# Feed-forward block and its two norms moved into the stage of the third relational layer; the last norm moved into the graph and attention output stage, both by node tiles

## What is computed

```python
xn = _layernorm(x)
x = x + relational_gnn(xn) + linear_attention_0(xn)     # three relational layers, the last is:
#   h3 = relu(sum_r mean_over_edges_of_r(h2 @ w_rel3[r]) + h2 @ w_root3 + b3), x = x + h3
x = x + ffn(_layernorm(x))       # 768 -> 192 -> 768, new_gelu, weights scaled by mixed coefficients
xn = _layernorm(x)
x = x + graph_conv(xn) + linear_attention_1(xn)         # attention ends in a norm with gamma, beta
x = x + experts(_layernorm(x))   # one shared expert, and two of eight routed ones for each token
```

## Time and profile before

| | us |
|---|---|
| median of three runs | 2197.76 |
| the profiled execution, its own time | 2203.24 |
| its span in the trace | 2201.5 |
| end of `g3` on TensorE to start of `m1` | 943.1 to 1044.2 |
| last graph product of `p1` to start of `rs` | 1382.4 to 1403.5 |

### The profile page before, as it was taken

One profiled execution on the slowest core, in us unless ns is written; L12 is line 12 of the kernel. 1 busy time (PEld: TensorE's weight loads), 2 busy tenths in 40 slices (PEclk: granted clock), 3 DMA queues, 4 the chain that ended last, 5 costly groups with the idle time before them and its releaser, 6 DMA issues. The chain is left out here.

```text
span 2201.5 us, 33777 instructions
## 1 busy us (share of the span) xinstructions
PE 2006.6 (91%) x13496; PEld 1892.4 (86%) x13496; DVE 1327.5 (60%) x1873; ACT 942.4 (43%) x1150; POOL 90.6 (4%) x70
## 2 busy tenths in 40 slices
PE   5899889999999999935999889799979999999996
PEld 4899879999999999935999879699968888888885
DVE  8455566444334343365357646562368888898886
ACT  6345412221222111111366632321157777777775
POOL 0000000000000000000001000000000101001001
PEclk9999899999999999967999979799989999999998
DMA  2310134220211121110310040412279999999997
GB/s 82 102 29 30 58 100 101 67 56 29 84 51 49 51 58 44 44 29 5 105 29 29 1 136 15 165 44 101 72 288 385 383 385 372 369 370 371 372 376 265
DMA packets 186687, 314.00 MB, mean 143 GB/s; under 512 B 13051, under 2 KB 87291, under 8 KB 186160
## 3 DMA queue, kind: packets, MB, share of 16 engines
q1 hardware_dynamic: 181488, 295.70, 38.5%
q0 software_dynamic: 4816, 16.62, 3.3%
q10 hardware_dynamic: 272, 0.07, 0.0%
HBM read 293.87 MB, written 20.40 MB: 143 GB/s over the span
## 5 line engine op out<-in xcount | busy, mean ns | idle before, releaser
L183 PE MATMUL psum<-re_whi,xt_sb 128*128 128x512 f32 (+1 forms) x1680 | 507.8, 377 | 1.5 <-DVE xt_sb L2889 1.5
L183 PE MATMUL psum<-ring_hi,xt_sb 128*128 128x256 f32 (+3 forms) x1920 | 357.5, 285 | 11.9 <-DVE m_v L701 3.9
L183 PEld LDWEIGHTS psum<-re_whi,xt_sb 128*128 128x128 f32 x1680 | 313.1, 189 | 47.1 <-issue 1.9
L2873 DVE TENSOR_TENSOR re_wlo<-moe_raw,re_whi 128x1536 fp32r<-128x1536 f32 x173 | 303.3, 1755 | 34.3 <-ACT re_whi L2827 33.8
L183 PEld LDWEIGHTS psum<-ring_hi,xt_sb 128*128 128x128 f32 (+1 forms) x1920 | 302.7, 190 | 13.1 <-issue 5.2
L183 PE MATMUL psum<-re_wlo,xt_sb 128*128 128x512 f32 (+1 forms) x840 | 313.5, 373 | 0.0
L2827 ACT ACTIVATE re_whi<-moe_raw 128x1536 fp32r<-128x1536 f32 x174 | 258.6, 1489 | 90.8 <-PE psum L183 88.9
L183 PE MATMUL psum<-ring_lo,xt_sb 128*128 128x256 f32 (+3 forms) x960 | 272.5, 284 | 0.0
L183 PEld LDWEIGHTS psum<-ring_lo,xt_sb 128*128 128x128 f32 (+1 forms) x960 | 182.4, 190 | 0.0
L183 PEld LDWEIGHTS psum<-re_wlo,xt_sb 128*128 128x128 f32 x840 | 159.0, 189 | 22.1
L2873 DVE TENSOR_TENSOR re_wlo<-re_more,re_whi 128x1536 fp32r<-128x1536 f32 x84 | 147.5, 1756 | 30.4 <-ACT re_whi L2827 30.4
(11 more groups left out here) (404 smaller groups left out, 3240.7 us busy)
## 6 DMA issues: line engine op xcount, KB each, us to landing
moe_raw<-in_L_ffn_Wg_r SPq DMA_DIRECT2D x74, 768.0 KB, 8.7
moe_raw<-in_L_ffn_Wu_r SPq DMA_DIRECT2D x58, 768.0 KB, 8.4
moe_raw<-in_L_ffn_Wd_r SPq DMA_DIRECT2D x42, 768.0 KB, 6.0
re_more<-in_L_ffn_Wd_r SPq DMA_DIRECT2D x42, 768.0 KB, 9.3
re_more<-in_L_ffn_Wu_r SPq DMA_DIRECT2D x30, 768.0 KB, 7.7
ring_raw<-in_L_gnn_w_rel SPq DMA_DIRECT2D x18, 896.0 KB, 5.0
re_more<-in_L_ffn_Wg_r SPq DMA_DIRECT2D x15, 768.0 KB, 7.2
ring_raw<-in_L_mix_W_qkv SPq DMA_DIRECT2D x24, 384.0 KB, 4.3
```

The costliest lines, as they stand in the source:

```text
L183: mm = pe.matmul(out, lhs[a], rhs[b], start=(first and i == 0), stop=(last and i == 2))
L2873: dve.tensor_tensor(wlo[:, i % RING, :], raw[i % RAWS], whi[:, i % RING, :].bitcast(F32), ALU.subtract)\
```

## The change

Three phases between the third layer and the attention (`n1`, `f0`, `n2`) go, and `n3` goes. Their work is written into `g3` (now `phase_last_layer_ffn`) and `p1`.

In `g3`, the feed-forward weights are loaded at its start by SP, ahead of the ring's loads, two of the DMAs behind a new wait on `inv_read`. Their transposes are cut into seven pieces, which run one after each of the jobs 3 to 9; ACT scales and rounds each piece straight from PSUM and DVE takes the rest. The bias of the second product becomes a 97th row of its weights, with a row of ones in the hidden part. Statistics for the norm are taken by cut. The last R and G2 are reordered by node tile (`LAST_ROWS`). The norm goes in two parts (tiles 0 to 2, tiles 3 and 4), and scaling moves from DVE to ACT (`Identity` with a shift). The hidden part is made in four units (384 or 244 columns, two halves of the hidden features), whose gelu starts with a Square and an Identity on ACT instead of two steps on DVE. Each output tile is followed by its statistics, and the second norm again goes in two parts.

```diff
-def phase_rgcn_out(k, name, h_in, bias):
+PREP_AT = 3
+PREPS = 7
+PARTS = ((0, 3), (3, TT))
+CUT = 3 * P
+UNITS_H = ((0, CUT, 0), (0, CUT, 1), (CUT, NT, 0), (CUT, NT, 1))
+LAST_ROWS = [("R", 0), ("R", 1), ("R", 2), ("G", 0), ("G", 1), ("G", 2), ("R", 3), ("R", 4), ("G", 3), ("G", 4)]
+def phase_last_layer_ffn(k, name, h_in, bias, w_fc, b_fc, w_proj, b_proj, alpha_e, alpha_r):
...
+            sp.wait_ge(s["inv_read"], 1)
+            sp.dma_start(bp[HP:HP + 1, :], b_proj.rearrange("(o d) -> o d", o=1)).then_inc(s["ffn_in"], 16)
+            sp.dma_start(fc, w_fc.rearrange("(g p) d -> p g d", p=HP)).then_inc(s["ffn_in"], 16)
             stream_loads(sp, st)
...
+            for t in range(3, TT):
+                root_tile(LAST, t)
+            message_tile(LAST, 2, 3)
+            turn_node(0)
+            message_tile(LAST, 2, 4)
+            turn_node(1)
+            turn_node(2)
+            hidden(0)
+            turn_node(3)
+            turn_node(4)
+            for u in range(1, 4):
+                hidden(u)
+            for i in range(2 * TT):
+                ffn_out(i)
+            for t in range(TT):
+                turn_out(t)
...
+            for t in range(3):
+                ffn_tile(t)
+            scale2(0)
+            ffn_tile(3)
+            low2(0)
+            ffn_tile(4)
+            scale2(1)
+            for t in range(1, TT):
+                low2(t)
```

```diff
+            sp.wait_ge(s["adj_made"], 1)
+            sp.wait_ge(s["deg_mm"], 1)
+            load_shared(sp, k, shared_sources(*shared, 0), 0, 0, 0)
+            for t, r0, r1 in ROWS:
+                sp.wait_ge(s["xn3_ready"], t + 1)
+                sp.dma_start(k.xn_dram[t * P + r0:t * P + r1, :], y_sb[r0:r1, t, :]).then_inc(s["kept"], 16)
+            sp.wait_ge(s["kept"], 16 * len(ROWS))
...
+            for t in range(3):
+                out_tile(t)
+            scale(0)
+            out_tile(3)
+            low(0)
+            out_tile(4)
+            scale(1)
+            for t in range(1, TT):
+                low(t)
```

More of the change, by code:

```diff
@@ new lines, in message_tile @@
+            def message_tile(c, r, t):
+                i = g_at[c, r, t]
+                if i >= 4:
+                    pe.wait_ge(s["g_read"], i - 3)
+                for u in range(TT):
+                    for a in range(2):
+                        mm = pe.matmul(g_bank(i)[0:TS[t], 0:W], k.C[0:TS[u], r, u, t * P:t * P + TS[t]],
+                                       y[0:TS[u], y_at[c, r] % 2, u, a, :],
+                                       start=(u == 0 and a == 0), stop=(u == TT - 1 and a == 1))
+                mm.then_inc(s["g_mm"], 1)
@@ new lines, in root, with normal @@
+            def root(n):
+                t0, t1 = PARTS[n]
+                act.wait_ge(s["mv_ready"], t1)
+                act.activation(k.root[:, t0:t1], k.mv[:, t0:t1, 1], ACT.Sqrt, bias=eps[:, 0:1]).then_inc(s["root_ready"], 1)
+            def normal(n):
+                t0, t1 = PARTS[n]
+                act.wait_ge(s["shift_made"], n + 1)
+                for t in range(t0, t1):
+                    ts = TS[t]
+                    if t >= 3:
+                        act.wait_ge(s["turned"], t - 2)
+                    act.activation(xn(t)[0:ts, :], k.x[0:ts, t, :], ACT.Identity, bias=k.shift[0:ts, t:t + 1],
+                                   scale=k.rstd[0:ts, t:t + 1]).then_inc(s["xn_ready"], 1)
@@ new lines, in normal2, with high2 @@
+            def normal2(n):
+                t0, t1 = PARTS[n]
+                act.wait_ge(s["shift2_made"], n + 1)
+                for t in range(t0, t1):
+                    ts = TS[t]
+                    act.activation(k.a[0:ts, t, :], k.x[0:ts, t, :], ACT.Identity, bias=k.shift[0:ts, t:t + 1],
+                                   scale=k.rstd[0:ts, t:t + 1]).then_inc(s["xn2_ready"], 1)
+            def high2(t):
+                act.wait_ge(s["turned2"], t + 1)
+                turned_high(act, k, t, turn2_banks(t)).then_inc(s["t2_hi"], 1)
@@ new lines, in _ @@
+                if kind != "G" and 4 * c + r + RING_SLOTS <= len(st.chunks):
+                    ring_low(dve, st, 4 * c + r + RING_SLOTS)
+                if n == PREP_AT - 1:
+                    coefficients()
+                if PREP_AT <= n < PREP_AT + PREPS:
+                    weights_low(n - PREP_AT)
+                if n == PREP_AT + PREPS:
+                    edge_rows()
+            for t in range(3):
+                root_sum(LAST, t)
+            for t in range(3):
+                last_message(t)
@@ L2112, in _ @@
                                    scale=k.rstd[0:TS[t], t:t + 1]).then_inc(s["normed"], 1)
+            act.wait_ge(s["eps_set"], 1)
+            root(0)
+            normal(0)
+            for t in range(3):
+                high(t)
+            root(1)
+            normal(1)
+            for t in range(3, TT):
+                high(t)
         @block.vector
```

717 lines of the change are left out of this document (435 added, 282 removed).

## The result

The changed kernel takes **2144.86 us** (median of 4 runs, 2136.58 to 2149.91) beside 2197.97 for the kernel before on the same chip: ratio 0.974, 95% interval 0.9709 to 0.9771. The forecast was 2138.5, with a range of 2130 to 2153. In two later measurements, on chips 13 and 1, the difference of the medians was 51.2 and 54.9 us; here it is 53.1.

What follows compares the result with a forecast made beforehand. No engine fills the 100.2 us of norms and feed-forward block: a chain where one works while others wait. Gains of 51.1 (first stage) and 8.2 (second) make 59.3; 2197.76 - 59.3 = 2138.5 us, range 2130 to 2153.

Steps and rivals of the forecast that it cites:

- T to the attention: From TensorE's start on the third layer's last root products (T) to the first attention matmul: 117.8 us becomes 62.7.
- The walk: First stage, step by step through three engines' new instruction lists: last transposes, copies and rests end at T + 60.3.
- The 2.0 for clock and hand-overs: First stage, added for transposes partly at the lower clock at the norms' ends and for hand-overs: 2.0 us.
- Weight transposes: Ahead of T, 24 transposes on a full TensorE: 3.5 to 5.6 us, taken as 4.0.
- I cost them at nothing.: Ahead of T, VectorE's weight pieces, coefficients and statistics of two cuts: 0; 7 us if cover fails at every piece.
- cover fails: Rival: VectorE's added layer work shows on TensorE (7), late chunk (3), `kept` costs more (3): 2151.5 us; chance 0.10.
- Second stage: First graph product to first router product: 41.7 us becomes 33.5, a gain of 8.2.
- `kept`: Second stage, SyncE's wait for saves to land: through at + 33.2, half a microsecond behind VectorE; 3 us more at worst.
- My row: Second stage, nearest profile row used for the saves' landing: a 64 KB load took 3.0 us.
- Table load: Ahead of the first tanh on ScalarE: 1.28 us, now on the path; the skill page's figure is 2.66 per switch.
- Behind the seam: Shared expert's second chunk, loaded later: ready 12.0 us after the seam, TensorE needs it at 13.0; nothing taken, at worst 3.
- The sum: Whole kernel: gains of 51.1 and 8.2 make 59.3 us, giving 2138.5 against the median; chance 0.62.

Runs made afterwards that it cites:

- e4: Changed kernel plus extra matmuls, whose results nobody reads, in TensorE's waits of the third layer's last part; median 2145.99 us, ratio 0.9753 to the kernel before.
- e9: Changed kernel with the seven weight preparation pieces and the edge row put back on the path, ahead of the scale; median 2163.92 us, ratio 0.9826 to the kernel before.
- e6: Changed kernel with the three one-partition edge row steps moved from behind job 10 to behind job 14; median 2142.0 us, ratio 0.973 to the kernel before.
- e8: Changed kernel with each of the seven groups of weight transposes issued three times, 48 transposes more; median 2151.4 us, ratio 0.9771 to the kernel before.
- e5: Changed kernel with one more single-column Tanh on ScalarE, moving the table load into an earlier wait; median 2142.42 us, ratio 0.9728 to the kernel before.
- e3: Changed kernel with the order by node tiles undone and both norms in one part of five tiles; median 2153.55 us, ratio 0.9785 to the kernel before.
- e10: Changed kernel with filled gaps, early table load, late edge row, tile 4 first in the second stage, extra matmuls ahead of graph products; 2135.98 us, ratio 0.9712.

## Why the prediction was right, point by point

- **T to the attention.** Forecast 62.7, measured 62.41, 62.42 and 62.42. The walk had 60.3 at the upper clock, and e4, with the gaps filled, has 60.06. The 2.0 for clock and hand-overs was a guess of about the right size: e4 prices the clock at 2.4. With the gaps filled the output products start at T + 35.7, where the walk has 35.6.
- **Weight transposes.** 4.0 forecast, 2.7 by e9 and e6, below the lower bound of 3.5. The unit was wrong: six transposes into an empty engine (0.87), whose row holds the tail of the last one. On a full engine each costs 0.096 (e8).
- **"I cost them at nothing."** Coefficients, statistics and pieces did hide. The edge row stands in no term of the prediction, and it cost 3.2 (e6). The rival "cover fails" had up to 7 at the seven pieces; the wait came one job behind the last of them. Together the layer grew by 6.4 instead of 4.0; that the transposes were priced 1.3 too high covered a part of what was missing, which is luck.
- **Second stage.** 33.5 forecast, 30.2 in the profile. At equal products, 20.56 + 12.35 = 32.9, a gain of 8.8 for the forecast 8.2. `kept` cost nothing: the issue of the last save ended at 1345.59 and SyncE waited 2.0 us for the saves, to 1347.6, while VectorE ended at 1348.49:

```profile
1333.98 11.61 SPq L2263 DMA_DIRECT2D xn_dram<-p_y  x6
...
1346.50 1.99 DVE L1602 TENSOR_TENSOR xt_sb<-psum,xt_sb 128x512 fp32r<-128x512 f32 x4 [1.74 <-ACT xt_sb L1594]
```

  My row, 3.0 for a load of 64 KB, was too long for this wait. The 2.0, behind a last save of 3 KB, agrees with the figure of the Trainium skill, DMA: Bandwidth & Descriptors, "Anatomy of one DMA", given with the prediction, though that section is about DMAs issued by GpSimd and these are SyncE's.
- **Table load.** It takes its 1.28 us of ScalarE and no more: the tanh starts at 970.52, where the load that began at 969.22 ends, and it began where the copies ended (969.20). The drain of about 1.38 us that the Trainium skill, ScalarE: Activation LUTs, "What ACT_TABLE_LOAD costs", adds does not appear here; the measurement decides. The prediction had the 1.28 fully exposed; taking it off the path shortened the stretch by only 0.7 (e5).
- **Behind the seam.** TensorE's first up product follows the gate products without a wait, at 1362.43, 13.6 us behind the router product's start; forecast 13.0. From the router product on the kernel takes 798.5 us beside 798.0, so nothing of the gain was given back there.
- **The sum.** By the stages 55.4 + 8.8 - 6.4 = 57.8 us are gained, forecast 59.3. The medians show 51.2, 53.1 and 54.9. The forecast time, 2138.5, was 6.4 us below the measured 2144.86. In the pair of profiles the difference lies in stages without an edit: the three of them took 1874.4 us before and 1880.7, 1875.0 and 1867.7 in the changed kernel. Over all thirteen profiles of the changed kernel and its variants they average 1873.9, so no lasting loss is to be seen there. Where the 3 to 7 us between the stages' sum and the medians lie stays open; there is no second profile of before.

## What to carry to other kernels

Where a phase is a chain through three engines, look first for what in it waits for nothing but its place: loads that could be issued earlier (VectorE sat 8.96 us for them here) and preparation that could run elsewhere (17 to 23 us, 12 to 17 net). The order by tiles comes after that (3 to 8). What joining the phases gives by itself wasn't measured; with the earlier loads and all that was rewritten on the way it is 30 us. Work moved onto a "half idle" engine is free only where nobody waits for what is queued behind it: the place in its list decides, and two microseconds of one-partition steps cost 3.2 between a split and the sums that free banks. Compare changed stages mark by mark, not medians, when untouched stages swing by 10 us and more; and see whether two profiles are level just ahead of the edit, for in e8 1.07 of the 5.67 us stood there already.

## What the runs showed of the hardware that I had not expected

- The same code with the same waits came out up to 8.6 us apart between executions of one kernel (beginning 765.50 and 756.92). In the two compared above, 5.9 of 6.5 us arose in 30 us that ran at a granted clock of 0.64 in one and 0.89 in the other.
- The same wait of 1.71 us was followed by 5.2 us for the next 30 matmuls in eight profiles and by 3.6 in a ninth, e3, with the same code at this place.
- Matmuls that do nothing are worth their place in a gap: 12 of them in 2.45 us of idle time brought the product behind them from 4.94 to 3.36 us.
- The ten graph products took 17.84 to 20.61 us in thirteen profiles behind the same idle time of 3.2 us, at a granted clock of 1.00 to 0.85. With the gap filled (e10) they took 17.86, as in four of the thirteen.
